# A two-layer graph network on one core: node tables of the second layer in two float32r parts instead of three bf16 parts

## The reference

```python
h = relu(layernorm(x))                       # layer 0
m = relu(h[dst']) + 1e-7                     # message per edge
h0 = segment_sum(m * edge_softmax(beta * m)) # per node
x = x + relu(h0 @ W1 + b1) @ W2 + b2
h = relu(layernorm(x))                       # layer 1
e = concat([h[src], h[dst], edge_attr])      # 96 per edge
v = relu(e @ W1 + b1) @ W2 + b2              # 32 per edge
x = x + maximum(segment_max(v, dst), h)
```

## Time and profile before

| | us |
|---|---|
| median of 3 runs | 1010.72 (1007.73 to 1011.56) |
| the profiled execution | 1012.41 |
| its span, first to last instruction | 1010.2 |
| PE busy in the span | 869.3 (86%) |
| DVE busy | 786.0 (78%) |
| POOL busy | 572.2 (57%) |
| ACT busy | 356.4 (35%) |
| the second layer's steps, L918 of the first to the last transpose | 400 to 964 |
| the rest: node maxima, output | 964 to 1010 |

### The profile page before, as it was taken

How to read it: one execution, slowest core, us unless ns; L and a number is a source line. 1 busy time by engine, 2 the same in 40 slices (tenths; PEclk the granted TensorE clock), 3 DMA queues, 4 the chain that set the end, 5 groups by cost and what they waited for, 6 DMA issues and landing times.

```text
span 1010.2 us, 22792 instructions
## 1 busy us (share of the span) xinstructions
PE 869.3 (86%) x5909; PEld 366.3 (36%) x5909; DVE 786.0 (78%) x1948; ACT 356.4 (35%) x911; POOL 572.2 (57%) x589
## 2 busy tenths in 40 slices
PE   1379999998988737999999999999999999999900
PEld 0133334433333413444444444444444444444300
DVE  7979999898979695877877777787777777776731
ACT  1489999887877100111111111111111111112100
POOL 3021111135431547777777777777777777777555
PEclk9989999988989668999999999999999999999965
DMA  3396889955655064454444455444445544444211
GB/s 96 107 117 111 116 108 113 110 85 93 99 91 101 8 114 99 130 149 135 119 119 124 114 140 144 133 121 116 124 116 134 148 132 126 114 116 135 59 30 26
DMA packets 130556, 110.47 MB, mean 109 GB/s; under 512 B 59866, under 2 KB 112190, under 8 KB 130524
## 3 DMA queue, kind: packets, MB, share of 16 engines
q1 hardware_dynamic: 103420, 87.51, 39.0%
q0 software_dynamic: 17120, 9.36, 6.6%
q10 hardware_dynamic: 9984, 13.22, 5.6%
HBM read 66.24 MB, written 16.85 MB: 82 GB/s over the span
## 4 chain that ended last, share of the span: by engine, by line
PE 75%; DVE 6%; ACT 6%; POOL 4%; DMA 4%; issue 4%; another core or an unknown queue 0%; DVEq 0%; POOLq 0%; SPq 0%; ACTq 0%
PE ps L891 37%; PE ps L781 12%; PE ps L791 6%; PE ps L926 5%; PE ps L915 5%; PE ps L918 5%; PE ps L908 4%; DMA cnt<-cg 2%; POOL cand L639 2%; POOL rows L630 2%; ACT cg L660 2%; ACT oh_act L669 2%; ACT lo_dist L667 2%; DVE onehot L1072 1%; DMA h_dram<-h 1%
## 5 line engine op out<-in xcount | busy, mean ns | idle before, releaser
L630 POOL DMA_INDIRECT rows<-h_dram,srcq_i x442 | 448.1, 1014 | 146.5 <-issue 134.4
L891 PE MATMUL ps<-grow,gs 128*128 128x448 bf16 (+1 forms) x988 | 200.2, 358 | 10.1 <-DVE grow L1132 10.1
L1072 DVE TENSOR_SCALAR onehot<-lo_iota,keys 128x392 f16<-128x392 f16 x706 | 188.6, 316 | 23.9 <-PE ps L781 19.8
L781 PE MATMUL ps<-onehot 128*128 128x391 f16 x706 | 167.3, 349 | 22.0 <-DVE onehot L1072 19.2
L725 ACT ACTIVATE scan_bufs<-scan_bufs 128x512 f32<-128x512 f32 (+1 forms) x52 | 32.0, 616 | 402.3 <-DVE scan_bufs L1174 402.3
L578 POOL DMA_INDIRECT grow<-g_dram,gidx x34 | 36.7, 1079 | 226.6 <-PE ps L791 180.6
L891 PE MATMUL ps<-onehot,gs 128*128 128x448 bf16 x780 | 156.4, 353 | 0.0
L660 ACT ACTIVATE cg<-ps 128x391 bf16<-128x391 f32 x269 | 129.7, 493 | 34.7 <-PE ps L781 20.9
L891 PEld LDWEIGHTS ps<-grow,gs 128*128 128x128 bf16 (+1 forms) x988 | 93.7, 99 | 123.5 <-issue 44.5
L1182 DVE STREAM_TRANSPOSE layer_in<-rows 32x288 f32<-32x288 f32 (+1 forms) x208 | 94.1, 453 | 51.5 <-DMA rows<-h_dram,srcq_i 46.2
L1066 DVE TENSOR_TENSOR onehot<-win_iota,keys 128x384 f16<-128x384 f16 x269 | 112.0, 416 | 1.5 <-issue 0.7
(11 more groups left out here) (204 smaller groups left out, 790.3 us busy)
## 6 DMA issues: line engine op xcount, KB each, us to landing
keys<-k_dram SPq DMA_DIRECT2D x26, 896.0 KB
cnt<-cg SPq DMA_DIRECT2D x205, 97.8 KB
rows<-h_dram,srcq_i POOLq DMA_INDIRECT x442
dstb<-in_dstw SPq DMA_DIRECT2D x26, 256.5 KB
layer_in<-in_eat ACTq DMA_DIRECT2D x104, 64.0 KB
v_dram<-vrow SPq DMA_DIRECT2D x26, 256.0 KB
grow<-cg SPq DMA_DIRECT2D x64, 97.8 KB
dstb<-in_dstw SPq DMA_DIRECT2D x26, 240.5 KB
```

Source lines behind the costliest of these rows:

```text
L630: gp.indirect_dma_start(rows[:, 2 * (it % 2) + i, t * D:t * D + D], None, h_dram[:, :], bass.IndirectOffsetOnAxis(srcq_i[:, col + t:col + ...
L781: nc.tensor.matmul(ps_cnt[:, (u // GT) % 4, 0:LO], oh_win[:, (u // GT) % RING_W, :, u % GT], moving, start=(u % GT == 0), stop=(u % GT == ...
L891: last = nc.tensor.matmul(ps[0][:, 2 * i + b, 0:KEY_BANK], hq[0:rows_, grp, t, :], oh_src[i][grp][0:rows_, KEY_BANK * b:KEY_BANK * b + KEY ...
L1072: V.tensor_scalar(oh_lo[:, u % RING, :], lo_iota[:, :], key_lo[:, ds(2 * CT * it + u, 1)], None, ALU.is_equal).then_inc(s_onehot, 1)
```

## The change

- h and the sums for `b_dram` are split into two float32r parts: the high part keeps the value's upper bits (a bitwise and that clears the low 12), the low part is the difference. `hq`, `wins`, the source one-hots and `ohd` become float32r, `b_dram` f32.
- `PC` becomes (8, 8), `PT` (8, 7): TensorE gathers 16 tiles a step, GpSimd 15. `KEY_BANK` becomes 512, a one-hot 128 x 1024, `hg` 1024 wide, the key table 1024 KB a step.
- A gather takes two matmuls a bank and group, the last group one (64 rows, at partition 0 for half 0 and 64 for half 1): 26 matmuls a half. L908 goes from six to four.
- Groups 0 and 1 of the seven one-hots are made by ScalarE in two activations each, Square(key_id - key) and Relu(1 - that); VectorE makes five.
- On ScalarE `source_onehots(it + 1, 1)` stands behind `hidden(it, 0)` and `source_onehots(it + 2, 0)` behind `hidden(it, 1)`, ahead of `features` and `limits`. Before the steps, those of step 0 and of the first half of step 1 stand behind `limits(0, 0)` and `limits(0, 1)`.
- TensorE takes gather groups 0 to 3 ahead of `outputs` and 4 to 6 behind it.
- Buffers of the second layer are placed over those of the first by a helper (`in_place_of`); some scratch tiles move.

The diff, without the placing of buffers:

```diff
-PC = (7, 7)
+PC = (8, 8)
...
+ACT_GROUPS = (0, 1)
+DVE_GROUPS = KEY_GROUPS - len(ACT_GROUPS)
+HIGH_BITS = -(1 << 12)
...
-        b_dram = nc.dram_tensor("b_dram", (512 * NB4, 3 * H), bf16).ap()
+        b_dram = nc.dram_tensor("b_dram", (512 * NB4, 2 * H), f32).ap()
...
+            [("hq", [P, KEY_GROUPS, 2, P], f32r), ("wins", [P, 2, 2, 2, P], f32r), ("src_dist", [P, len(ACT_GROUPS), slot], bf16)])
...
+            [("ohd0", [P, w_all[0]], f32r), ("ohd1", [P, w_all[1]], f32r), ("limits", [P, 4 * 512], f32)])
...
+            [(f"oh_src{n}", [P, slot], f32r) for n in range(2 * FULL + 1)])
...
+        oh_src = [[oh_all[FULL * i + n][:, :] for n in range(FULL)] + [oh_all[2 * FULL][:, :]] for i in range(2)]
+        LAST = [slice(64 * i, 64 * i + 2 * D) for i in range(2)]
...
-            for t in range(3):
+            for t in range(4):
                 sp.dma_start(last_f[D * t:D * t + D, :].rearrange("p (b c) -> p b c", b=4),
...
             for i in range(2):
                 limits(0, i, True)

-            def hidden_step(it, first, last=False):
+            def source_onehots(it, par, i, first=False):
+
+                act.wait_ge(s_keyb[par], 8 * it - 8 * par + 16)
+                if not first:
+                    act.wait_ge(s_gat[i], it)
+                for n, grp in enumerate(ACT_GROUPS):
+                    if i == 1 or not first:
+                        act.wait_ge(s_ohs_act[1 - i], len(ACT_GROUPS) * (it - 1 + i) + n + 1)
+                    nc.scalar.activation(src_dist[:, n, :], keyb[par][:, 0, KEY_AT[i]:KEY_AT[i] + slot], ACT.Square, scale=-1.0, bias=key_id[:, grp:grp + 1]).then_inc(s_src_dist, 1)
+                    act.wait_ge(s_src_dist, len(ACT_GROUPS) * (2 * it + i) + n + 1)
+                    nc.scalar.activation(oh_src[i][grp], src_dist[:, n, :], ACT.Relu, scale=-1.0, bias=ones[:, 0:1]).then_inc(s_ohs_act[i], 1)
+
+            for i in range(2):
+                source_onehots(0, 0, i, True)
+            source_onehots(1, 1, 0)
+
+            def hidden_step(it, par, first, ahead=2):
                 for i in range(2):
                     hidden(it, i, first)
-                    if not last:
+                    if i == 0 and ahead >= 1:
+                        source_onehots(it + 1, 1 - par, 1)
+                    if i == 1 and ahead == 2:
+                        source_onehots(it + 2, par, 0)
+                    if ahead >= 1:
                         features(it + 1, i)
                         limits(it + 1, i, False)
...
-                    pe.wait_ge(s_ohs[i], KEY_GROUPS * it + grp + 1)
-                    parts, rows_ = (range(3), P) if grp < FULL else (range(1), 3 * D)
+                    if grp in ACT_GROUPS:
+                        pe.wait_ge(s_ohs_act[i], len(ACT_GROUPS) * it + ACT_GROUPS.index(grp) + 1)
+                    else:
+                        pe.wait_ge(s_ohs[i], DVE_GROUPS * it + grp - sum(a < grp for a in ACT_GROUPS) + 1)
+                    parts, rows_ = (range(2), slice(0, P)) if grp < FULL else (range(1), LAST[i])
...
-                for t in range(3):
+                for t in range(2):
                     for s in range(2):
                         nc.tensor.matmul(ps[1][:, 2 * i + s, 0:w], wins[64 * s:64 * s + 64, i, s, t, :], ohd[i][64 * s:64 * s + 64, :],
...
-                        gather(it + 1, i, 0, 3, False)
+                        gather(it + 1, i, 0, 4, False)
                     outputs(it, i)
                     if beside:
-                        gather(it + 1, i, 3, KEY_GROUPS, False)
+                        gather(it + 1, i, 4, KEY_GROUPS, False)
...
                 for grp in range(KEY_GROUPS):
-                    V.tensor_scalar(oh_src[i][grp], keyb[par][:, 0, KEY_AT[i]:KEY_AT[i] + slot], key_id[:, grp:grp + 1], None, ALU.is_equal).then_inc(s_ohs[i], 1)
+                    if grp in ACT_GROUPS:
+                        continue
+                    part_ = slice(0, P) if grp < FULL else LAST[i]
+                    V.tensor_scalar(oh_src[i][grp][part_, :], keyb[par][part_, 0, KEY_AT[i]:KEY_AT[i] + slot], key_id[part_, grp:grp + 1], None, ALU.is_equal).then_inc(s_ohs[i], 1)
...
-            step(V.tensor_copy(sq[:, :, :], h[:, :, :]))
-            three_parts([hq[:, 0:FULL, t, :] for t in range(3)], sq[:, 0:4 * FULL, :].rearrange("p (g b) c -> p g (b c)", b=4)).then_inc(s_h3, 1)
+            step(high(sq[:, 0:4 * FULL, :], h[:, 0:4 * FULL, :]))
+            V.tensor_copy(hq[:, 0:FULL, 0, :], full[1])
+            V.tensor_tensor(hq[:, 0:FULL, 1, :], full[0], full[1], ALU.subtract).then_inc(s_h3, 1)
             ve.wait_ge(s_bmm, 1)
-            step(V.tensor_copy(bf, ps[1][:, :, :].rearrange("p a b -> p (a b)")[:, 0:NB4 * 4 * H]))
-            three_parts([b3[:, :, t, :] for t in range(3)], bf.rearrange("p (m c) -> p m c", c=H)).then_inc(s_b3, 1)
+            step(high(b2[:, :, 0, :], b_sum))
+            V.tensor_tensor(b2[:, :, 1, :], b_sum, b2[:, :, 0, :], ALU.subtract).then_inc(s_b3, 1)
```

More of the change, by code:

```diff
@@ L1 @@
+import math
 from contextlib import ExitStack
@@ L76, in build @@
           beta, w01, b01, w02, b02, w11, b11, w12, b12, out):
-    f32, f16, bf16, i32 = mybir.dt.float32, mybir.dt.float16, mybir.dt.bfloat16, mybir.dt.int32
+    f32, f16, bf16, i32, f32r = mybir.dt.float32, mybir.dt.float16, mybir.dt.bfloat16, mybir.dt.int32, mybir.dt.float32r
     ALU, ACT, AX = mybir.AluOpType, mybir.ActivationFunctionType, mybir.AxisListType.X
@@ L83, in sb, with in_place_of @@
             return ctx.enter_context(nc.sbuf_tensor(name, shape, dt))
+        def in_place_of(first, second):
+            with ExitStack() as early:
+                before = [early.enter_context(nc.sbuf_tensor(name, shape, dt)) for name, shape, dt in first]
+            after = [sb(name, shape, dt) for name, shape, dt in second]
+            taken = [sum(math.prod(shape[1:]) * (2 if dt in (f16, bf16) else 4) for _, shape, dt in some) for some in (first, second)]
+            if taken[0] > taken[1]:
+                sb(first[0][0] + "_rest", [P, (taken[0] - taken[1] + 3) // 4], f32)
+            return before + after
         def sem(name):
@@ L181, in build @@
         dstb = [sb(f"dstb{i}", [P, 32 * HALF[i] + 1], i32) for i in range(2)]
[L182 to L187, removed]
-        grow_flat = grow[:, :, :].rearrange("p a b -> p (a b)")
[L189 to L198, removed]
+        same, lim = ([limits_[:, 1024 * n + 512 * i:1024 * n + 512 * i + 32 * HALF[i]] for i in range(2)] for n in range(2))
+        ohd = [ohd0[:, :], ohd1[:, :]]
+        grow_flat = grow[:, :, :].rearrange("p a b -> p (a b)")
+        oh_src = [[oh_all[FULL * i + n][:, :] for n in range(FULL)] + [oh_all[2 * FULL][:, :]] for i in range(2)]
+        LAST = [slice(64 * i, 64 * i + 2 * D) for i in range(2)]
+        keyb = [keyb0, keyb1]
         w1s4 = sb("w1s4", [P, H], f32)
@@ L213, in build @@
         hg = tmp_flat[:, 0:4 * KW]
-        last_f = tmp_flat[0:3 * D, 4 * KW + 128:4 * KW + 256]
-        last_p = tmp_flat[0:3 * D, 4 * KW + 256:4 * KW + 448].bitcast(bf16).rearrange("p (t c) -> p t c", t=3)
-        assert 4 * KW + 448 <= 3 * NB * D and 4 * KW + 128 >= 2 * ((E - 1) // 127)
+        last_f, last_h = (tmp_flat[:, 4 * KW + 128 * n:4 * KW + 128 * n + 128] for n in range(2))
+        assert 4 * KW + 256 <= 3 * NB * D and 4 * KW >= 2 * ((E - 1) // 127)
         kr = 4 * STEPS
@@ L220, in build @@
         sk_lo = hid[0][0:kr, 1, 0:KW].bitcast(i32)
[L221 to L222 removed]
+        rows_flat = rows[:, :, :].rearrange("p a c -> p (a c)")
+        sk_row, sk_hi = (rows_flat[0:kr, KW * n:KW * n + KW].bitcast(i32) for n in range(2))
         sk_m, sk_key = run[0][0:kr, 0:KW], vrow[0][0:kr, 0:KW]
[L224 removed]
+        key_out = res[:, :, :].rearrange("p k c -> p (k c)")[0:kr, 0:KW].bitcast(f16).rearrange("p (k c) -> p k c", k=2)
         last0_i = sb("last0_i", [1, GROUPS], i32)
@@ L322, in build @@
         s_lim = [sem(f"s_lim{i}") for i in range(2)]
+        s_ohs_act = [sem(f"s_ohs_act{i}") for i in range(2)]
+        s_src_dist = sem("s_src_dist")
         s_ohs = [sem(f"s_ohs{i}") for i in range(2)]
@@ L1134, in _, with high @@
             after_mlp(0)
[L1136 to L1141, removed]
-                return V.tensor_copy(parts[2], value)
+            def high(part_, value):
+                return V.tensor_scalar(part_.bitcast(i32), value.bitcast(i32), HIGH_BITS, None, ALU.bitwise_and)
@@ L1157, in _ @@
+            step(high(last_h, last_f))
+            for i in range(2):
+                V.tensor_copy(hq[64 * i:64 * i + D, FULL, 0, :], last_h[64 * i:64 * i + D, :])
+                done_ = V.tensor_tensor(hq[64 * i + D:64 * i + 2 * D, FULL, 0, :], last_f[64 * i + D:64 * i + 2 * D, :], last_h[64 * i + D:64 * i + 2 * D, :], ALU.subtract)
             done_.then_inc(s_h3, 1)
```

63 lines of the change are left out of this document (34 added, 29 removed).

## The result

The changed kernel takes **978.47 us** (median of 4 runs, 973.92 to 979.34) against 1011.14 for the kernel before, run on the same chip: ratio 0.967, 95% interval 0.962 to 0.971. The profiled execution took 978.41 us, its span is 976.6. The forecast was 985 us, range 952 to 1012, faster.

The account below looks back on a forecast made before the run. TensorE bounds the kernel now; afterwards VectorE's loop through the key and destination transfer sets 21.2 us a step. 414.6 + 23 x 21.2 = 902.2, end 938.6 against 964.1, so -25.5: 986.9, less 1.7 for the median: 985 us, range 952 to 1012.

Parts of the forecast that it names:

- The ring: VectorE's loop through one-hots, L1190, then keys and destinations on SP's queue; to set 21.2 us a step, chance 0.55.
- Own part: VectorE's share of the loop, from destinations arriving to the next keys' issue: 12.93 + 0.77 = 13.7 us a step.
- Transfer: Keys with destinations behind them on SP's queue, until VectorE's L1173 starts: 7.0 to 9.0 us, 7.5 taken.
- 5.8 + 0.47: TensorE's gathers per half, 26 matmuls at 0.223 us, plus windows cut from three parts to two (0.71 x 2/3).
- 2.6 us to give: TensorE's slack a step, needing 18.6 us where the loop through the key transfer takes 21.2.
- the predicted stall of 2 us a step ahead of the outputs: TensorE's output matmuls wait for ScalarE's hidden layer, queued behind limits that wait for destinations; about 2 us, costing nothing.
- Rival B: GpSimd's tiles, not the transfer, set the pace at 20.1 us a step: 960 us; chance 0.19.
- Rival C: Edge transfers collide with destinations, transfer 8.3 to 9.0 us, step 22.0 to 22.7, 1005 to 1022 us; chance 0.12.
- Rivals D and E: D: float32r streams at half rate, about 1230 us, chance 0.08. E: one-hots write one element a cycle, about 1065, 0.06.
- a limit of the port: TensorE's moving operand limited to about 614 GB/s: 4-byte columns at half rate, 0.43 us a gather matmul.
- The lower bound of 1.05: Low end for one ScalarE activation of 1024 elements, between 1.05 and 1.62 us; 1.15 taken.
- Start and end: First gather near 392, L1173 of step 1 at about 414.6, step 24 to 25 18.7 us, last transpose 938.6.

Follow-up runs that it names:

- cut_low: Changed kernel without the low part of two full groups, 8 fewer gather matmuls a step; 975.69 us, ratio 0.960 to the kernel before.
- feat_mid: Changed kernel with ScalarE's four edge transfers of a half issued between its first and second one-hot; 997.39 us, ratio 0.984 to the kernel before.
- dst_first: Changed kernel with half 0's destination transfer issued ahead of the next step's keys on SyncE's queue; 963.39 us, ratio 0.953 to the kernel before.
- pc7_f32r: Changed kernel with the old split back, 14 tiles on TensorE and 17 on GpSimd; 995.7 us, ratio 0.986 to the kernel before.
- cut_low_dst_first: dst_first without the low part of two full groups, 8 fewer matmuls a step; 939.27 us, ratio 0.927 to the kernel before.
- act_one: Changed kernel with one one-hot of each half moved from ScalarE back to VectorE; 1013.21 us, ratio 1.003 to the kernel before.

## Why the prediction was right, step by step

- **The bound.** The ring of VectorE and the key and destination transfer is what the step follows: it is the chain in the trace, taking work off TensorE changes little (cut_low), and a transfer made longer by timing alone costs 19 us (feat_mid, 997.39 against 978.47; by the ratios 17).
- **The ring's two terms.** Own part 13.7 forecast, 13.53 measured: one-hots came 0.66 us apart as taken ((3.40 - 0.75)/4). Transfer 7.5 forecast, 7.18 measured. Over 23 steps 20.77 for 21.2, 415.2 + 477.8 = 893.0 for 902.2: 9.2 us less than forecast, of which the last step gives 2.6 back, and the rest is the difference between 985 and 978. The edges were to stand 4 us behind the keys and stood 2; the 7.5 was picked between 7.0 and 9.0 on that ground, and feat_mid, whose edges go out 2.2 us earlier, has 8.23. That they did not fall there was lucky.
- **TensorE was mis-sized.** A gather matmul takes 3.94/16 = 0.246 us, not 0.223, and in the runs of 9 it is 2.49/9 = 0.277 (dst_first's chain). Two things are in this: inside a run one starts 0.234 us behind the other (median of the starts in 430 to 900 us), and the first of a run takes 0.34, where the kernel before, with 448 columns, had 0.189 and 0.20; the short runs have more of the second. Gathers and windows are 7.11 us a half where the forecast had 5.8 + 0.47. TensorE needs 20.1 to 20.2 us a step, not 18.6. It had not 2.6 us to give but half a microsecond. The time did not suffer, because the ring was still longer, and that was luck: 0.6 us more a step and TensorE would have been the pace. But the predicted stall of 2 us a step ahead of the outputs was 0.3 (7.4 us in all), and taking the destinations off the ring could bring no more than 0.58 us a step.
- **GpSimd** was taken at 20.1 us for 15 tiles; it did 17 in 21.5 (pc7_f32r) and 15 in 19.1 (cut_low_dst_first). Rival B (960 us) had the wrong engine: with the transfer out of the way it is TensorE that sets 20.1, and dst_first's 963 looks like B for another reason.
- **Rival C was near.** act_one and feat_mid are its mechanism, a little milder than the 8.3 to 9.0 us and 22.0 to 22.7 a step that it had: edges within 0.3 us of the keys, transfer 8.1 to 8.2 on average, steps 22.3 and 21.8, 1013 and 997 us. The changed kernel escapes it by the 2 us that ScalarE's one-hots happen to put between them.
- **Rivals D and E** are out: 0.246 us a matmul is short of 0.27, and 0.66 us a one-hot is half of 1.2. The 0.43 us a matmul that a limit of the port would have given did not appear: 4-byte columns do not go at half rate.
- **ScalarE.** Square and Relu take 1.14 and 1.15 us (1.15 taken). The lower bound of 1.05 rested on 0.84 ns an element, which 630 and 600 ns do not give: 30/32 = 0.94, so a bound of 1.11.
- **Start and end.** First gather 390.3 (392), L1212 of step 1 at 415.2 (414.6), step 24 to 25 18.7 (18.7), the last step 20.3 (17.7; where the 2.6 come from stays open), so 932.0 against 938.6.

## What to carry to other kernels

When a change unloads the bounding engine, write down the closed loops that pass through a transfer and add their links: by the forecast's sum the loop (21.2 us) was within 0.8 us of TensorE's step of 22.04, and it took over at once. Small transfers that an engine needs soon go ahead of the large one on the queue: a reorder that was worth nothing while TensorE was full was worth 1.5% after it. And a kernel whose time hangs on where one queue's transfers fall against another's can lose 2% by an edit that looks unrelated, as by giving ScalarE less to do; compare the two issue times before blaming the edited instruction.

## What the runs showed of the hardware

- Float32r matmuls are a tenth slower by column than bf16, over runs of 16 to 18: 448 columns took 0.215 us against 0.195, and 512 took 0.246. Part of it is the first of a run, 0.34 us against 0.20. Their weights load in 189 ns each (page of the changed kernel). The forecast had 0.14, but that is the spacing of L820's matmul records; the weight loads of that line took 186 to 338 ns each in the same trace.
- A broadcast of 1024 KB and 256 KB behind it took 6.66, 7.18 or 8.23 us on average, by the moment alone at which four small transfers on another queue were issued (2.2 us ahead, 2.1 behind, 0.2 ahead).
- GpSimd's indirect transfers have no fixed pace: 1.265 us a tile where they were the bound, 1.34 where TensorE was, with no wait between them in either. The trace of dst_first shows with what the length goes: a tile that begins beside a transpose, the scan, L1236 (the mask) or an idle VectorE takes 0.94 to 0.95 us, one beside the one-hots of L1178 1.09 on average, one beside L1220 1.22. No run tests this by itself.
